# Attention outputs turned, normalised and turned back by VectorE's 32x32 transposes

## Chip, cores and metric

One core of one Trainium2 chip. The metric is the device time of one execution in microseconds (us), a median of several runs. PE is TensorE, ACT is ScalarE, DVE is VectorE, POOL is GpSimd, SP is SyncE, which here only issues DMAs.

## What is computed

One transformer block on 32 batches of 128 tokens with 128 channels: modulated layer norm, self attention with 16 heads of 8 channels, a gated projection added to x, cross attention to 77 context tokens, its projection added to x, and an MLP of 512 hidden channels with its own modulation and gate. Cut to what matters here:

```python
attn_w = softmax(einsum('bhqd,bhkd->bhqk', q, k) * scale)
attn_out = einsum('bhqk,bhkd->bhqd', attn_w, v)            # divided by the sum of the exponentials
x = x + gate_a * (attn_out.transpose(0,2,1,3).reshape(B,N,H) @ W_proj + b_proj)
...                                                        # cross attention the same way, without a gate
x = x + gate_m * (gelu(modulate(ln(x)) @ W_mlp1 + b_mlp1) @ W_mlp2 + b_mlp2)
```

The softmax's division is done after the product with v: the v operand carries a column of ones for each head, so that each head gives 8 unnormalised outputs and the sum of its exponentials.

## The kernel before

**Slots, beats, pairs.** The batches go in 16 pairs. The attention part is a software pipeline of slots -2 to 19. Within a slot `here` is the pair whose self attention begins, `back1` (called `d`) the one before it, whose self attention is finished and projected, `back3` (`e`) the one whose cross attention is finished, `back4` (`z`) the one whose cross output is projected and added. Slots 4 to 13 are a loop of two slots an iteration, the others are written out. Each slot has 8 beats `t`; each engine has its own in-order list of work for each beat, written out by hand in the function `slot` of its block, and engines wait for each other by counting semaphores. After the slots comes the MLP, in 8 groups of 4 batches.

**The scores.** In each beat PE computes one unit of scores (8 heads of one batch) for the row maxima, self attention in beats 0 to 3 and cross attention in beats 4 to 7 (`scores`, L1111), into `ps_max`, which has one buffer. DVE takes the maxima (`maxima`, L736) and PE may write the next unit when DVE is done. In the same way PE computes transposed scores (L1122) into `ps_st`, also a single buffer, and ACT takes their exponentials (L895). PE multiplies the exponentials with v (`values`, L1133) into `ps_o`, one bank for the four units of a pair.

**What is done with `ps_o`.** It holds, for each of 4 groups of 32 partitions, 2 heads times 16 rows (8 outputs, the sum, 7 unused), and 128 queries in the columns of each unit. For self attention of pair `d`:

- beat 1: ACT copies `ps_o` (128x512) to `sum` (`sums`, L916), which frees `ps_o` for the cross units from beat 2 on
- beat 2: PE turns it by four 128x128 transposes into the bank `o_t` (`flip_sums`, L1208)
- beat 3, ahead of that beat's maxima: DVE takes the reciprocal of the sums (L743) and multiplies (L747), from PSUM to `o` with queries in the partitions
- beat 3: PE turns `o` back by two transposes (`flip_out`) into the bank `ob_t`
- beat 4: ACT copies that to `oT` (L923), and PE projects (L1347), DVE adds (L753, `residual`), and after the maxima of beat 5 takes the statistics of the new x (L698), POOL the reciprocal root (L525), and in beat 6 DVE normalises (L714, `normalise`), PE turns it (L1200, `x1_t`), ACT copies it, and in beat 7 PE computes the cross queries (L1221)

Cross attention of pair `e` has the same five steps: sums in beat 5 (after which `ps_o` is free for self units from beat 6 on), `flip_sums` in beat 6, reciprocal and multiply in beat 7 ahead of the maxima, `flip_out` in beat 7, copy to `ocT` in beat 0 of the next slot, then the projection (L1307).

**DMAs.** The q and k operands of the scores are three-way bf16 splits, made by POOL (L530 to L544) and stacked into `qk_st` and `qkc_st` by six DMAs of 128 KB for each pair, issued by SP (L372). Cross queries computed in beat 7 are split, stacked and wanted by PE in beat 4 of the next slot.

**Weights.** The rows of `w_proj` and `w_cproj`, and of two bias columns, are loaded in an order (`o_rows`) that fits the order in which the flips leave the heads; each of these loads is two DMAs.

Of the kernel before, what the change touches and what calls it, by code (L numbers as in the profile page):

```python
# [24 lines left out]
B, T, C = 32, 128, 128  # L25
# [3 lines left out]
G = 2  # L29
# [46 lines left out]
def ring(*streams):  # L76
# [10 lines left out]
        ("max_s0", "here", 2), ("o_t", "back1", 1),  # L87
        ("ob_t", "back1", 2), ("ctx_t", "back1", 0), ("v", "ahead", 1),
        ("max_s1", "here", 0), ("proj", "back1", 2),
        ("kv_c", "back1", 1),  # L90
        ("max_c0", "back2", 0), ("oc_t", "back3", 1), ("x1_t", "back1", 2), ("x_t", "far", 2),
        ("q_c", "back1", 0), ("obc_t", "back3", 1)]
# [91 lines left out]
def block_kernel(nc, x, cond, ctx, w_mod, b_mod, w_qkv, b_qkv, w_proj, b_proj, w_qc, b_qc, w_kvc, b_kvc,  # L184
# [5 lines left out]
    with es:  # L190
# [112 lines left out]
        for name in ("cond_in w_in wm_in wq_in bm_in bd_in b_in bc_in b1_in w12_in wc_in x_in0 x_in1 x_in2 x_in3 x_in4 c_in0 c_in1 c_in2 c_in3 c_in4 z_pool z_dve zq_set zk_set zv_set zvc_set "  # L303
# [4 lines left out]
                     "smax_ps smaxc_ps st_ps stc_ps pv_ps pvc_ps ot_ps obt_ps oct_ps obct_ps "  # L308
# [23 lines left out]
        def hold(eng, name, value):  # L332
# [46 lines left out]
        def _(sp):  # L379
            def o_rows(src):  # L380

                return src.rearrange("(j r m) c -> r j m c", r=2, m=2 * D)

# [20 lines left out]
            for r in range(2):  # L404
                sp.dma_start(wcproj_sb[r * C // 2:(r + 1) * C // 2], o_rows(w_cproj)[r]).then_inc(sems["w_in"], 16)
# [229 lines left out]
        def _(dve):  # L635
# [103 lines left out]
            def attention_out(p, kind, job, ready, rden_name, name, taken):  # L739

                src = ps_misc[BANK[job]][:].rearrange("q (r m x) -> q r m x", r=2 * G, x=2 * D)
                w(dve, ready, p.n + 1)
                nc.vector.reciprocal(att[kind]["rden"][:], src[:, :, :, D]).then_inc(sems[rden_name], 1)  # L743
                if not p.first():
                    w(dve, taken, p.n)
                w(dve, rden_name, p.n + 1)
                nc.vector.tensor_tensor(att[kind]["o"][:], src[:, :, :, 0:D],  # L747
                                        att[kind]["rden"][:].unsqueeze(3).to_broadcast([T, 2 * G, 8, D]),
                                        ALU.mult).then_inc(sems[name], 1)
# [39 lines left out]
            def slot(s):  # L789
                far, a, h, d, f, e, z = (s.pair(n) for n in ("far", "ahead", "here", "back1", "back2", "back3", "back4"))  # L790
                for t in range(BEATS):
# [24 lines left out]

                    if t == 0 and far:
# [45 lines left out]
        def _(act):  # L863
            def o_rows(src):

                return src.rearrange("(j r m) c -> r j m c", r=2, m=2 * D)

# [13 lines left out]
            for r in range(2):  # L881
                act.dma_start(wproj_sb[r * C // 2:(r + 1) * C // 2], o_rows(w_proj)[r]).then_inc(sems["w_in"], 16)
            with nc.allow_non_contiguous_dma(reason="bias columns"):
                for n, (src, at) in enumerate(((b_qkv, 2 * C), (b_kvc, C))):
                    for r in range(2):
                        act.dma_start(bv_sb[r * C // 2:(r + 1) * C // 2, n:n + 1],
                                      o_rows(src[at:at + C].rearrange("(c o) -> c o", o=1))[r]).then_inc(sems["b_in"], 16)
# [15 lines left out]
            def empty_max(p, b, job, ready, dst, name, loaded):  # L903
                w(act, ready, 2 * p.n + b + 1)
                if not p.first():
# [3 lines left out]
                                     ACT.Copy).then_inc(sems[name], 1)  # L909

            def sums(p, kind, src, ready, name, taken):

                w(act, ready, NU * p.n + NU)
                if not p.first():
                    w(act, taken, p.n)
                nc.scalar.activation(att[kind]["sum"][:].rearrange("c b r q -> c (b r q)"), src[:, :],  # L916
                                     ACT.Copy).then_inc(sems[name], 1)
# [38 lines left out]
            def slot(s):  # L956
                a, h, d, f, e, z = (s.pair(n) for n in ("ahead", "here", "back1", "back2", "back3", "back4"))
                for t in range(BEATS):
# [7 lines left out]
                    if t == 0 and z:  # L966
                        copy(ocT[:], ps_misc[BANK["obc_t"]][:, 0:GT], "obct_ps", z, "ocT_set", "projc_ps")
# [27 lines left out]
                    if t == 4 and d:  # L995
                        copy(oT[:], ps_misc[BANK["ob_t"]][:, 0:GT], "obt_ps", d, "oT_set", "proj_ps")
# [29 lines left out]
                    if t == 1 and d:  # L1026
                        sums(d, "s", ps_o, "pv_ps", "sum_set", "ot_ps")
# [15 lines left out]
                    if t == 5 and e:  # L1043
                        sums(e, "c", ps_o, "pvc_ps", "sumc_set", "oct_ps")
# [38 lines left out]
        def _(pe):  # L1083
# [107 lines left out]
            def slot(s):  # L1191
# [10 lines left out]

                def flip(job, p, srcs, ready, counted):

                    dst = bank(s, job)
                    w(pe, ready, p.n + 1)
                    for n, src in enumerate(srcs):
# [232 lines left out]
```

## Time and profile before

| | us |
|---|---|
| median of 3 runs | 406.55 |
| the runs | 403.11, 406.55, 407.51 |
| span of the profiled execution | 401.9 |
| busy in the span: PE, ACT, DVE, POOL | 336.8, 268.8, 257.0, 216.6 |

The span runs from the first instruction to the last of one profiled execution. The time of that execution as the runs count it isn't given; the median of the runs is 4.65 us above its span, the lowest run 1.2 us. Attention fills the span up to about 340 us, the MLP the rest.

### The profile page before, as it was taken

How to read it: one execution, taken by the hardware profiler on the slowest of the kernel's cores; microseconds unless marked ns; L12 is line 12 of the kernel's file. 1: busy time of each engine (PE TensorE's matmuls, PEld its weight loads, DVE VectorE, ACT ScalarE, POOL GpSimd, SP SyncE). 2: the span in 40 equal slices, each digit the busy share in tenths (PEclk: the TensorE clock that was granted, in tenths of full speed). 3: DMA queues.
4: the chain of work that ended last, by engine and by line, in shares of the span. 5: the costliest groups of instructions: out<-in, count | busy, mean ns of one | idle time of the engine just before them, and what ended most of it. 6: DMA issues, size and time to landing. Idle time of an engine off the chain costs nothing.

```text
span 401.9 us, 16368 instructions
## 1 busy us (share of the span) xinstructions
PE 336.8 (84%) x6072; PEld 227.1 (56%) x6072; DVE 257.0 (64%) x650; ACT 268.8 (67%) x523; POOL 216.6 (54%) x494
## 2 busy tenths in 40 slices
PE   3474875989889999999999899988678778999994
PEld 3342553666666767667677677766545434454442
DVE  5754665768779788788887888868625441424401
ACT  1244563868778888887888878877573465677672
POOL 7824475867676686777777777756344210211200
PEclk9997799999999999999999999999997599999998
DMA  5244467253343543435425343353130300001101
GB/s 154 52 105 108 125 151 166 55 136 85 85 97 82 119 106 81 102 85 126 99 68 123 81 116 94 81 123 78 36 82 4 81 2 2 26 26 41 39 26 52
DMA packets 65549, 33.15 MB, mean 82 GB/s; under 512 B 8359, under 2 KB 65255, under 8 KB 65511
## 3 DMA queue, kind: packets, MB, share of 16 engines
q1 hardware_dynamic: 61983, 31.77, 32.7%
q10 hardware_dynamic: 3528, 0.86, 1.1%
q8 instruction: 25, 0.41, 0.4%
q14 instruction: 13, 0.11, 0.1%
HBM read 4.83 MB, written 2.10 MB: 17 GB/s over the span
## 4 chain that ended last, share of the span: by engine, by line
PE 41%; DVE 16%; issue 16%; SPq 9%; DMA 8%; ACT 4%; POOL 2%; ACTq 1%; DVEq 1%; POOLq 0%
PE ps_o L1180 7%; DMA qkc_st<-qkcp 7%; SPq L372 7%; PE ps_o L1133 6%; PE wide L1172 6%; PE wide L1111 5%; DVE x_n L714 3%; PE wide L1122 3%; DVE mxc L736 3%; DVE mx L736 2%; SPq L412 2%; DVE x_stats L698 2%; PE ps_misc L1200 2%; PE ps_misc L1208 2%; PE ps_misc L1221 2%
## 5 line engine op out<-in xcount | busy, mean ns | idle before, releaser
L895 ACT ACTIVATE p_c<-wide 128x1024 f32<-128x1024 f32 x64 | 65.6, 1026 | 36.5 <-PE wide L1122 36.1
L736 DVE TENSOR_REDUCE mx<-wide 128x8 f32<-128x1024 f32 x64 | 78.0, 1218 | 18.4 <-PE wide L1111 18.2
L895 ACT ACTIVATE p_s<-wide 128x1024 f32<-128x1024 f32 x64 | 65.7, 1026 | 11.8 <-PE wide L1122 11.0
L736 DVE TENSOR_REDUCE mxc<-wide 128x8 f32<-128x616 f32 x64 | 51.0, 797 | 27.5 <-PE wide L1111 26.4
L1133 PE MATMUL ps_o<-p_c,vc_m 128*32 128x128 f32 x1024 | 43.0, 287 | 0.8 <-ACT p_c L895 0.6
L1133 PE MATMUL ps_o<-p_s,v_m 128*32 128x128 f32 x1024 | 42.5, 285 | 0.6
L1111 PE MATMUL wide<-qk_st 62*128 62x128 bf16 x512 | 26.5, 225 | 11.6 <-DVE mx L736 9.7
L1111 PE MATMUL wide<-qkc_st 62*128 62x77 bf16 x512 | 20.8, 204 | 14.2 <-DMA qkc_st<-qkcp 13.4
L1111 PEld LDWEIGHTS wide<-qk_st 62*128 62x128 bf16 x512 | 15.1, 97 | 29.3 <-DVE mx L736 23.7
L1133 PEld LDWEIGHTS ps_o<-p_s,v_m 128*32 128x32 f32 x1024 | 25.1, 111 | 8.4 <-issue 3.1
L1172 PE MATMUL wide<-m_nT,w_sb 128*128 128x512 f32 x64 | 29.6, 597 | 0.2 <-DVE mxc L736 0.2
L1133 PEld LDWEIGHTS ps_o<-p_c,vc_m 128*32 128x32 f32 x1024 | 25.0, 112 | 8.0 <-issue 0.9
L1122 PE MATMUL wide<-qkc_st 64*128 64x128 bf16 x512 | 26.0, 221 | 3.6 <-ACT p_c L895 3.3
L1180 PE MATMUL ps_o<-qk_st,w_sb 128*128 128x512 f32 x64 | 28.9, 594 | 0.0
L1122 PE MATMUL wide<-qk_st 64*128 64x128 bf16 x512 | 26.4, 224 | 2.7 <-ACT p_s L895 1.4
L561 POOL CAST nmc<-mxc 128x16 bf16<-128x16 f32 x32 | 6.3, 196 | 40.6 <-issue 26.8
L1111 PEld LDWEIGHTS wide<-qkc_st 62*128 62x128 bf16 x512 | 12.5, 98 | 26.7 <-issue 21.4
L567 POOL TENSOR_TENSOR m_ve<-m_mv,eps_sb 128x4 f32<-128x4 f32 x8 | 1.6, 200 | 47.9 <-DVE m_mv L772 47.9
L753 DVE TENSOR_TENSOR xs<-xs,ps_misc 128x256 f32 (+1 forms) x32 | 13.5, 421 | 17.4 <-PE ps_misc L1347 10.4
L786 DVE TENSOR_TENSOR m_out<-xs,ps_misc 128x512 f32<-128x512 f32 x8 | 5.5, 688 | 29.6 <-PE ps_misc L1188 29.6
L946 ACT ACTIVATE m_y<-ps_o,gb_m,mod 128x128 f32<-128x128 f32 x32 | 12.1, 457 | 18.0 <-PE ps_o L1180 18.0
L525 POOL TENSOR_TENSOR x_rstd<-x_ve,mhalf 128x2 f32<-128x2 f32 x32 | 22.4, 700 | 2.9 <-POOL x_ve L520 0.8
(152 smaller groups left out, 815.5 us busy)
## 6 DMA issues: line engine op xcount, KB each, us to landing
qkc_st<-qkcp SPq DMA_DIRECT2D x96, 128.0 KB, 2.6
qk_st<-qkp SPq DMA_DIRECT2D x94, 128.0 KB, 2.5
out<-m_out SPq DMA_DIRECT2D x8, 256.0 KB, 2.3
xs<-x SPq DMA_DIRECT2D x3, 512.0 KB, 4.9
qk_st<-nmT SPq DMA_DIRECT2D x64, 4.0 KB
qkc_st<-nmcT SPq DMA_DIRECT2D x64, 4.0 KB
ctx_sb<-ctx SPq DMA_DIRECT2D x3, 308.0 KB
w_sb<-L_xcond_W_mlp ACTq DMA_DIRECT2D x2, 256.0 KB, 3.1
```

Of the source, the lines that this page charges most:

```text
L372: queue.dma_start(dst[c:128:ROWSTEP], parts[:].rearrange("c a p t -> c (a p) t")[:, a:b + 4:b + 3 - a]).then_inc(sems[name], 16)
L525: nc.gpsimd.tensor_tensor(L["rstd"][:], L["ve"][:], mhalf[0:L["rows"], 0:G], ALU.pow).then_inc(sems[f"{kind}_rstd_set"], 1)
L714: last = nc.vector.tensor_scalar(L["xn"][:, b], src(b), L["mv"][:, b, 0:1], L["rstd"][:, b:b + 1], ALU.subtract, ALU.mult)
L736: nc.vector.reduce_max(mxt[:, b].rearrange("q (x r) -> q r x", r=2)[:, r], src, AX.X, negate=True).then_inc(sems[done], 1)
L753: nc.vector.tensor_tensor(xs[:, batches(p)], xs[:, batches(p)], ps_misc[BANK[job]][:, 0:GT].rearrange("t (b c) -> t b c", b=G), ALU.add).t ...
L895: nc.scalar.activation(dst[u % 2][:].rearrange("k x q -> k (x q)"), ps_st[:].rearrange("k s x -> k (s x)"), ACT.Exp, scale=SCALE).then_inc ...
L946: last = nc.scalar.activation(m_y[par][:, b * T:(b + 1) * T], ps_y[:, b * T:(b + 1) * T], ACT.Identity, bias=one(gb_m, g, b), scale=one(mo ...
L1111: last = mm(ps_max[:, s_, j * T:j * T + keys], st[p.par][lo:lo + KROWS, m, 0, b * T:(b + 1) * T], st[p.par][lo:lo + KROWS, m, 1, b * T:b * ...
L1122: last = mm(ps_st[:, s_, j * T:(j + 1) * T], st[p.par][lo:lo + HALF, m, 1, b * T:(b + 1) * T], st[p.par][lo:lo + HALF, m, 0, b * T:(b + 1) ...
L1133: last = mm(ps_o[32 * j:32 * j + 32, at:at + T], vt[p.par][:, b, 4 * j + 2 * r + s_], probs[u % 2][:, 4 * s_ + j], start=(s_ == 0), stop=( ...
L1172: mm(ps_h[k], w1_sb[:, k * 128:(k + 1) * 128], m_nT[par][:], start=True, stop=True).then_inc(sems["m_h_ps"], 1)
L1180: last = mm(ps_y[:, :], w2_sb[:, k], hT[par][:, k], start=(k == 0), stop=(k == NF - 1))
```

## The change

DVE takes over the turning. Its transpose instruction turns each 32x32 block by itself and leaves it within its 32 partitions. Since `ps_o` keeps each head's 16 rows within one group of 32 partitions, turning the blocks puts queries in the partitions for four groups of heads at once; after the division the same turn gives channels in the partitions, in the natural order of the heads. Per slot and kind of attention there are now three steps, all on DVE:

- `turn_sums`: one transpose of 128x512 f32 from `ps_o` to `sum` (beat 1 for self, beat 5 for cross, behind that beat's maxima). It frees `ps_o`
- `divide`: reciprocal of 128x32 and multiply of 128x256, both from SBUF (beats 2 and 6, behind the maxima)
- `turn_back`: one transpose of 128x256 f32 from `o` straight to `oT` or `ocT` (beats 3 and 7, ahead of the maxima)

PE loses `flip_sums` and `flip_out`, ACT loses `sums` and the copies to `oT` and `ocT`. Four PSUM jobs (`o_t`, `ob_t`, `oc_t`, `obc_t`) and the waits on their banks are gone. A unit's place in `ps_o` is now (2r+b) instead of (2b+r). `w_proj`, `w_cproj` and the bias columns are loaded in their natural order: 4 DMAs fewer at the start, 3 of them on ACT's queue.

```diff
-            def attention_out(p, kind, job, ready, rden_name, name, taken):
-                src = ps_misc[BANK[job]][:].rearrange("q (r m x) -> q r m x", r=2 * G, x=2 * D)
-                w(dve, ready, p.n + 1)
-                nc.vector.reciprocal(att[kind]["rden"][:], src[:, :, :, D]).then_inc(sems[rden_name], 1)
...
+            def turn_sums(p, kind, ready, name):
+                w(dve, ready, NU * p.n + NU)
+                nc.vector.transpose(att[kind]["sum"][:].rearrange("t (a r s) x -> t a r (s x)", r=2, s=2),
+                                    ps_o[:].rearrange("c (r a q) -> c a r q", r=2, q=32)).then_inc(sems[name], 1)
+            def divide(p, kind, ready, rden_name, name):
+                w(dve, ready, p.n + 1)
+                nc.vector.reciprocal(att[kind]["rden"][:], att[kind]["sum"][:, :, D]).then_inc(sems[rden_name], 1)
+                w(dve, rden_name, p.n + 1)
+                nc.vector.tensor_tensor(att[kind]["o"][:], att[kind]["sum"][:, :, 0:D],
+                                        att[kind]["rden"][:].unsqueeze(2).to_broadcast([128, 2 * G * T // 16, D]),
+                                        ALU.mult).then_inc(sems[name], 1)
+            def turn_back(p, kind, dst, ready, name, taken):
+                w(dve, ready, p.n + 1)
+                if not p.first():
+                    w(dve, taken, p.n)
+                nc.vector.transpose(dst[:], att[kind]["o"][:].rearrange("t m d -> t (m d)")).then_inc(sems[name], 1)
...
                     if t == 3 and d:
-                        attention_out(d, "s", "o_t", "ot_ps", "rden_set", "o_set", "obt_ps")
+                        turn_back(d, "s", oT, "o_set", "oT_set", "proj_ps")
                     if t == 7 and e:
-                        attention_out(e, "c", "oc_t", "oct_ps", "rdenc_set", "oc_set", "obct_ps")
+                        turn_back(e, "c", ocT, "oc_set", "ocT_set", "projc_ps")
...
+                    if t == 1 and d:
+                        turn_sums(d, "s", "pv_ps", "sum_set")
+                    if t == 2 and d:
+                        divide(d, "s", "sum_set", "rden_set", "o_set")
+                    if t == 5 and e:
+                        turn_sums(e, "c", "pvc_ps", "sumc_set")
+                    if t == 6 and e:
+                        divide(e, "c", "sumc_set", "rdenc_set", "oc_set")
...
-                    if t == 0 and z:
-                        copy(ocT[:], ps_misc[BANK["obc_t"]][:, 0:GT], "obct_ps", z, "ocT_set", "projc_ps")
...
-                    if t == 1 and d:
-                        sums(d, "s", ps_o, "pv_ps", "sum_set", "ot_ps")
...
-                at = u * T
+                at = (G * r + b) * T
...
-                    if t == 2 and d:
-                        flip_sums("o_t", "s", d, "sum_set", "ot_ps")
...
-                        flip_out("ob_t", "s", d, "o_set", "obt_ps")
```

## Rows read from the trace of the kernel before

**Rows 1.** The page: busy time (first line), chain that ended last, by engine and line.

```profile
PE 336.8 (84%) x6072; PEld 227.1 (56%) x6072; DVE 257.0 (64%) x650; ACT 268.8 (67%) x523; POOL 216.6 (54%) x494
PE 41%; DVE 16%; issue 16%; SPq 9%; DMA 8%; ACT 4%; POOL 2%; ACTq 1%; DVEq 1%; POOLq 0%
PE ps_o L1180 7%; DMA qkc_st<-qkcp 7%; SPq L372 7%; PE ps_o L1133 6%; PE wide L1172 6%; PE wide L1111 5%; DVE x_n L714 3%; PE wide L1122 3%; DVE mxc L736 3%; DVE mx L736 2%; SPq L412 2%; DVE x_stats L698 2%; PE ps_misc L1200 2%; PE ps_misc L1208 2%; PE ps_misc L1221 2%
```

**Rows 2.** Busy time by stretch: slots 3-5, 6-13, 14-15; stretch, length, engines, clock, DMA.

```profile
78.74:130.59 51.85, 46.19 (x1104) 34.43 (x1092) 40.82 (x97) 40.27 (x80) 36.98 (x85) 1.00 0.41 96
130.59:261.53 130.94, 122.95 (x2916) 91.76 (x2912) 109.39 (x253) 107.63 (x209) 97.14 (x223) 1.00 0.41 98
261.53:295.84 34.31, 28.03 (x683) 20.67 (x672) 22.73 (x47) 24.30 (x47) 19.17 (x49) 1.00 0.32 74
```

**Rows 3.** Timeline, DVE, beat 5 to the next: start, length, line, operation, count, idle before.

```profile
170.19 0.79 DVE L736 TENSOR_REDUCE mxc<-wide 128x8 f32<-128x616 f32 x1
170.90 0.48 DVE L698 BATCH_NORM_STATS2 x_stats<-xs 128x6 f32 x2
172.89 0.60 DVE L714 TENSOR_SCALAR x_n<-xs,x_mv,x_rstd 128x128 f32 x2
173.40 0.36 DVE L743 RECIPROCAL c_rden<-ps_misc 128x32 f32<-128x32 f32 x1
173.87 0.42 DVE L747 TENSOR_TENSOR c_o<-ps_misc,c_rden 128x256 f32<-128x256 f32 x1
174.36 0.80 DVE L736 TENSOR_REDUCE mxc<-wide 128x8 f32<-128x616 f32 x1
175.08 0.75 DVE L714 TENSOR_SCALAR ctx_n<-ctx_sb,ctx_mv,ctx_rstd 77x128 f32 x2
...
180.66 1.23 DVE L736 TENSOR_REDUCE mx<-wide 128x8 f32<-128x1024 f32 x1 [0.52 <-PE wide L1111]
182.05 0.36 DVE L743 RECIPROCAL s_rden<-ps_misc 128x32 f32<-128x32 f32 x1 [0.17 <-PE ps_misc L1208]
182.85 1.22 DVE L736 TENSOR_REDUCE mx<-wide 128x8 f32<-128x1024 f32 x1
184.79 0.80 DVE L736 TENSOR_REDUCE mxc<-wide 128x8 f32<-128x616 f32 x1 [0.72 <-PE wide L1111]
186.21 0.42 DVE L753 TENSOR_TENSOR xs<-xs,ps_misc 128x256 f32 x1 [0.62 <-PE ps_misc L1347]
```

**Rows 4.** Timeline, PE, the same slot: where PE waited for the maxima and for DMA.

```profile
177.91 0.40 PE L1111 MATMUL wide<-qk_st 62*128 62x128 bf16 x8 [0.26 <-DVE mx L736]
180.19 0.40 PE L1111 MATMUL wide<-qk_st 62*128 62x128 bf16 x8 [0.22 <-DVE mx L736]
...
184.34 0.32 PE L1111 MATMUL wide<-qkc_st 62*128 62x77 bf16 x8 [0.20 <-DMA qkc_st<-qkcp]
```

**Rows 5.** Groups by line: name, shapes, count, busy us, mean ns, idle us before.

```profile
L736 DVE TENSOR_REDUCE mx<-wide 128x8 f32<-128x1024 f32 x64 | 78.0, 1218 | 18.4 <-PE wide L1111 18.2
L786 DVE TENSOR_TENSOR m_out<-xs,ps_misc 128x512 f32<-128x512 f32 x8 | 5.5, 688 | 29.6 <-PE ps_misc L1188 29.6
L638 DVE MEMSET qk_st<- 128x1024 uint32 x2 | 1.8, 912 | 1.2 <-PEq L1430 1.0 <-issue 0.2
```

**Rows 6.** Busy time by stretch, early slots, for the granted clock; columns as in rows 2.

```profile
45.30:66.00 20.70, 14.42 (x253) 9.19 (x245) 13.64 (x30) 11.77 (x25) 15.94 (x35) 1.00 0.61 138
66.00:68.00 2.00, 0.39 (x17) 0.36 (x21) 0.02 (x1) 0.00 (x0) 1.05 (x1) 1.00 0.49 114
68.00:70.00 2.00, 1.80 (x49) 1.27 (x46) 1.80 (x3) 0.49 (x2) 0.00 (x0) 0.62 0.52 122
```

**Rows 7.** Timeline, all engines, slots 18 and 19, the last pair's cross attention output.

```profile
333.16 0.64 PE L1133 MATMUL ps_o<-p_c,vc_m 128*32 128x128 f32 x16 [0.57 <-ACT p_c L895]
...
335.58 0.60 ACT L916 ACTIVATE c_sum<-ps_o 128x512 f32<-128x512 f32 x1
...
336.32 0.63 PE L1208 MATMUL ps_misc<-ident,c_sum 128*128 128x128 f32 x4 [0.60 <-ACT c_sum L916]
```

More of the change, by code:

```diff
@@ L86 @@
         ("qk", "ahead", 0),
-        ("max_s0", "here", 2), ("o_t", "back1", 1),
-        ("ob_t", "back1", 2), ("ctx_t", "back1", 0), ("v", "ahead", 1),
+        ("max_s0", "here", 2),
+        ("ctx_t", "back1", 0), ("v", "ahead", 1),
         ("max_s1", "here", 0), ("proj", "back1", 2),
         ("kv_c", "back1", 1),
-        ("max_c0", "back2", 0), ("oc_t", "back3", 1), ("x1_t", "back1", 2), ("x_t", "far", 2),
-        ("q_c", "back1", 0), ("obc_t", "back3", 1)]
+        ("max_c0", "back2", 0), ("x1_t", "back1", 2), ("x_t", "far", 2),
+        ("q_c", "back1", 0)]
 BANK = {name: bank for name, _, bank in MISC}
@@ L403, in _ @@
             load_x(1)
-            for r in range(2):
-                sp.dma_start(wcproj_sb[r * C // 2:(r + 1) * C // 2], o_rows(w_cproj)[r]).then_inc(sems["w_in"], 16)
+            sp.dma_start(wcproj_sb[:], w_cproj).then_inc(sems["w_in"], 16)
             for dst, src in ((wqc_sb, w_qc), (wkvc_sb, w_kvc)):
@@ L908, in empty_max @@
                 nc.scalar.activation(dst[:, b], ps_misc[BANK[job]][:].bitcast(bf16)[0:2 * H, 0:T],
[L909 to L916, printed above, removed]
                                      ACT.Copy).then_inc(sems[name], 1)
@@ L1201, in transposed @@
                     last.then_inc(sems[counted], 1)
[L1203 to L1207, printed above, removed]
-                        last = tr(dst[:, n * 128:(n + 1) * 128], src, ident[:])
-                    last.then_inc(sems[counted], 1)
-                def flip_sums(job, kind, p, ready, counted):
-                    flip(job, p, [att[kind]["sum"][:, b, r] for b in range(G) for r in range(2)], ready, counted)
-                def flip_out(job, kind, p, ready, counted):
-                    flip(job, p, [att[kind]["o"][:, 2 * b:2 * b + 2].rearrange("q r m d -> q (r m d)") for b in range(G)],
-                         ready, counted)
                 def project(job, p, weights, src, ready, counted, cols=GT):
@@ L1364, in slot @@
                         max_t("max_c0", f, 0, nmc, "nmc_set", "mtc_ps")
-                    if t == 6 and e:
-                        flip_sums("oc_t", "c", e, "sumc_set", "oct_ps")
                     if t == 6 and far:
@@ L1373, in slot @@
                         project("q_c", d, wdh[:, 2], x1T[:], "x1T_set", "qc_ps")
-                    if t == 7 and e:
-                        flip_out("obc_t", "c", e, "oc_set", "obct_ps")
                     if h and h.first() and t < 2:
```

40 lines of the change are left out of this document (13 added, 27 removed).

## The prediction

> **What bounds the kernel now.** I read the page first. PE is busiest by far [rows 1], so a change that takes work off PE looks welcome. But the chain that ended last has only 41% on PE, and three things around it that aren't PE's arithmetic: DVE's maxima and statistics, SP's issue of the `qkc_st` stack, and that stack's flight. So I cut the span into slots by the starts of `sums` and asked for the busy time of each stretch. Slots 6 to 13 take 130.94 us, 16.37 us each; in such a slot PE is busy 15.37 us, DVE 13.67, ACT 13.45, POOL 12.1 [rows 2]. PE idles 1.0 us a slot and DVE 2.7.
>
> Whether PE's busy time sets that 16.37 I read from the timelines of DVE and of PE over one slot. DVE runs from the residual of beat 4 (the last row is the next slot's; this slot's lies 16.36 us earlier, at 169.85) to the maxima of beat 1, which end 0.52 ahead of the 180.66 row, at 180.14, with nothing between its operations but short waits on itself; neighbours overlap by 0.07 to 0.09 us, as 170.19 + 0.79 against 170.90 shows. After it come 0.52, 0.17, 0.72 and 0.62 us of waiting for PE [rows 3]. PE in turn waits for DVE's maxima at 177.91 and 180.19, and barely for the DMA at 184.34 [rows 4]. The reader is to see a chain that passes from DVE to PE and back: scores can't be written before the maxima of the unit ahead are taken, since `ps_max` has one buffer, and for 10.3 of 16.4 us DVE has no gap in which more work would be free. PE is nearly full, but over that stretch it is full because it has the time. A second loop is as long: cross queries in beat 7, split, six DMAs, scores in beat 4 of the next slot; the 0.20 us wait on DMA [rows 4] says that it closes at nearly the same moment.
>
> **What the change takes away.** On PE twelve transposes a slot: four take 0.63 us [rows 7], so 1.9 us of busy time. On ACT two copies of 0.60 us [rows 7] and two of half that size, 0.3 to 0.6 us each: about 2 us. On DVE the wait of 0.17 us for the flip [rows 3]. On POOL nothing. Neither PE's nor ACT's work lies on the path of the 10.3 us; what it would be worth there I count as nothing, because what bounds there is DVE. The cover for that is DVE's own queue; if it weren't full, the two `flip_sums` on PE would be worth 0.6 us each.
>
> **What it adds on DVE.** No row shows a DVE transpose. Nearest is a DVE operation from PSUM with the same 512 elements a partition, 688 ns (L786); the maxima with 1024 take 1218 ns [rows 5], so an element costs (1218-688)/512 = 1.04 ns and an operation 157 ns. By that `turn_sums` is 0.69 us and `turn_back` with 256 elements 0.42, the time of the multiply and residual of that size [rows 3]. Less the overlap of 0.08 they cost the queue 0.61 and 0.34 us. Ends of the range: a memset does 1024 words in 912 ns [rows 5], 0.89 ns each with nothing for the start, so 0.46 and 0.23 us, which I take as the low end; if a 4-byte element needs two passes, the 1024-element reduction gives 1.22 us, and the same 1.04 ns gives 0.69 us for 256 elements. I take the middle, since element counts and source are the same. `divide` keeps two operations; their source moves from PSUM to SBUF. They take 0.36 and 0.42 now; I leave them so. `turn_back` waits on the multiply directly in front of it in beat 6 to 7 and beat 2 to 3 (only `residual`-like work could stand between, and there is none), 0.1 us as between reciprocal and multiply (173.40 + 0.36 against 173.87).
>
> The Trainium skill (Vector Engine (DVE) Microarchitecture Reference, section 3.8) says that the transposing front end sustains one element per cycle and lane, and its page VectorE: DVE Perf Modes (section on the TRN2 errata) gives 120 cycles and one per element from PSUM, 58 from SBUF, at 0.96 GHz. By these figures, an estimate, the two would be 0.66 and 0.33 us in place of 0.69 and 0.42, and the forecast about 2 us lower. No run here shows it yet; the nearest row, 688 ns, is 30 ns above the page's figure for its size.
>
> **One slot walked through.** Cross half, beats 5 to 7 [rows 3]: `turn_sums` comes between the maxima at 170.19 and the statistics at 170.90. Its input, PE's last cross product, is queued on PE right behind the scores whose maxima DVE spends 0.79 us on, so I take it as ready when they end, and everything behind moves by 0.61: statistics, POOL's root, `x1_n` at 172.89, the cross queries. Reciprocal and multiply then fill 173.40 to 174.29 as before, and where the next maxima stood at 174.36 `turn_back` stands until 174.73: 0.37 more. From 175.08 to 180.14 DVE is full, so the 0.98 us arrive whole at beat 1. Self half: `turn_sums` follows the maxima of beat 1 and takes 0.61 us, and there the queue had a gap of 0.52 while PE makes the next scores: 0.01 to 0.1 more, counted as 0. PE's first cross product of beat 2 waits for it (`sum_set`), queued in front of the rest of that beat, but it is ready within 0.05 us of when ACT's copy would let it go. The reciprocal no longer waits 0.17, and `turn_back` comes before the maxima of 182.85: 182.05-0.24+0.36+0.10+0.42+0.10+0.34 = 183.13, so 0.28 more. The gaps of 0.72 and 0.62 are PE's own scores and projection, unchanged. Sum: 0.98 + 0 + 0.28 = 1.26 us, a slot of 17.6 us with DVE busy about 15.6.
>
> **The sum.** Slots 6 to 13: 8 x 1.26 = 10.1 us. Slots 3 to 5 and 14 to 15 take 17.2 us on average [rows 2]; in them I take the DMA loop as the longer one (SP's issue and the flight of `qkc_st` have 7% of the chain each, [rows 1]), which hides the self half, but `turn_sums` of cross attention stands in front of the cross queries and so inside that loop: 5 x 0.61 = 3.0. Slots 16 and 17, the same: 1.2. Slots 1 and 2 have only the self half, ahead of a DMA wait: 0. Slot 18 gives back: the last product ends at 333.80, but the last `c_sum` comes on ACT only at 335.58, behind work of the MLP, and PE waits 0.60 us for it and turns for 0.63 [rows 7]. DVE, idle there, needs 0.69 + 0.36 + 0.42 + 0.42 and three waits of 0.1, 2.2 us from 333.80, and has `ocT` at 336.0. PE's wait of 0.60, its flips of 0.63 and 0.3 and, in front of the projection, about another 0.5 of waiting for the copy go: 2.0 us less. At the start four DMA issues go; ACT's queue has 1% of the chain, 4 us at the most [rows 1], and the loads on it that the first steps need stand ahead of those: 0. Total 10.1 + 3.0 + 1.2 - 2.0 = +12.3: a span of 401.9 + 12.3 = 414.2 us. The median of the runs lies 4.65 above the span of the profiled one, so 406.55 + 12.3, about 419 us. POOL and SP get no work; with 1.26 us more in each slot their queues only wait longer.
>
> **Rivals.**
> (a) The transposes need two passes. `turn_sums` and `turn_back` cost 0.53 and 0.27 us more, 1.6 a slot for both halves: over the 14 slots 3 to 16 +22, so 441 us. For it: reciprocals of 32 elements in 0.36 us show that a DVE operation can cost far more than 1 ns an element. Against: nothing in the rows.
> (b) DVE and POOL get in each other's way. Two `ctx_n` of 128 elements take 0.75 us at 175.08, while POOL works, against 0.60 for two `x_n` [rows 3]. The multiply now reads two SBUF operands; 0.15 us on each of six operations a slot is up to 0.9, x 14 = +13: 432. The Trainium skill (GPSIMD Engine Reference, its specifications) has such contention for DVE operations with two SBUF inputs; by its rule the multiply, but not the transposes, is slowed. The 0.75 us is consistent with that, no more.
> (c) The clock. PE goes from 15.4 busy of 16.4 us to 13.5 of 17.6, 77%. The clock fell to 1.2 GHz after a stretch in which PE did 0.39 us in 2.0, and held at 2.4 with 14.42 busy in 20.70 us, 70% [rows 6]. No gap over 1.5 us is to come in a slot, so it should hold. If not, PE's operations take up to twice as long, some +1.5 us a slot: 14 x 1.5 = +21: 440.
> (d) The transposes are cheap (0.46 and 0.23 us). Then a slot grows by 1.26 - 0.23 - 2 x 0.19 = 0.65 us, and the cross half's share in the DMA loop is 0.38: 5.2 + 5 x 0.38 + 2 x 0.38 - 2.0 = +5.9: 412. If PE's relief hides some of that, as much as 0.3 us a slot, it is 409.
> (e) It gets faster: DVE's work fits in its gaps, and PE is what bounds. Place: the gaps of 0.52, 0.17, 0.72 and 0.62 us, 2.0 us a slot, against 1.9 added. Price: the four-transpose flip of each half leaves the chain; `ps_misc L1208` has 2% of it, 8 us [rows 1], and with the tail's 2 that is 396. It decides if the new work can start in the gaps; for three of the four it can't, since in the hand-written order the operation behind the gap is the one that waits.
>
> **Chances.** Forecast with its own range 414 to 425: 0.60. (a) 0.07, (b) 0.08, (c) 0.05, (d) 0.12, (e) 0.08. The measurement tells about 1% from no change, so faster is below 402.5 and slower above 410.6 us. Faster: (e), 0.08. Same: half of (d), and what of the forecast and of (b) PE's relief might bring there, 0.11 in all. Slower: 0.81. Range for 8 in 10: from 408, the low side of (d), to 432, the end of (b), leaving out (a), (c) and (e).
>
> **What would show it.** In the profile after: slots of 17.6 us in the loop; DVE transposes of 0.69 and 0.42 us; DVE busy 15.6 us a slot, PE about 13.5; PE's waits for `mx` and `mxc` grown by over 1 us a slot; the 0.52 us gap gone, those of 0.6 to 0.7 kept; clock 1.00 there. Wrong if transposes are far from 0.69, if the slot stays at 16.4 with full DVE (then DVE wasn't on the path), or if the DMA wait in beat 4 grows instead.

## The result and the profile after

The median of 4 runs is 438.88 us (436.53 to 439.64), against 404.83 for 4 runs of the kernel before: a ratio of 1.083 (1.076 to 1.089). The change costs 34 us where 12.3 were forecast, and the time lies outside the range. The profiled execution has a span of 437.3 us, 35.4 more than the 401.9 before. A few runs of each kernel fall into a slower state: the ratios leave them out, the medians don't, and the profiled execution of `self_only` is one of them.

The page of the kernel after: busy time, the granted clock in 40 slices, the chain by engine, and four of the costliest groups (line, engine, operation, count | busy us, mean ns | idle before).

```profile
PE 340.3 (78%) x5880; PEld 221.8 (51%) x5880; DVE 288.1 (66%) x714; ACT 247.2 (57%) x459; POOL 220.8 (50%) x494
PEclk9999796989896988989889898989996567899999
PE 44%; DVE 20%; issue 11%; SPq 10%; DMA 8%; ACT 3%; ACTq 1%; POOL 1%; DVEq 1%; POOLq 0%
L731 DVE TENSOR_REDUCE mxc<-wide 128x8 f32<-128x616 f32 x64 | 50.9, 795 | 32.6 <-PE wide L1102 32.4
L1191 PE MATMUL ps_misc<-ident,x_n 128*128 128x128 f32 x64 | 15.0, 328 | 32.0 <-DVE x_n L709 32.0
L1102 PE MATMUL wide<-qk_st 62*128 62x128 bf16 x512 | 28.4, 237 | 13.9 <-DVE mx L731 12.2
L1010 ACT ACTIVATE x1T<-ps_misc 128x256 f32<-128x256 f32 x16 | 6.2, 384 | 37.8 <-PE ps_misc L1191 37.8
```

Set against [rows 1], two lines don't fit a plain loss on VectorE. PE has 192 instructions fewer and is busy 3.5 us longer, so what is left of its work runs slower: the clock row dips to 8 in about half of the slices of the loop, where the page of before has a 9 in each slice there. And PE idles 32.0 us for `x_n`, the normalised input that it turns; before it was 6.5 us on the same line (L1200 there). So I looked at beat 6, where DVE normalises x1. The lines of the new and the kept operations, DVE:

```profile
L737 DVE STREAM_TRANSPOSE c_sum<-ps_o 128x512 f32<-128x512 f32 x16 | 11.3, 708 | 7.8 <-PE ps_o L1124 7.8
L737 DVE STREAM_TRANSPOSE s_sum<-ps_o 128x512 f32<-128x512 f32 x16 | 11.3, 706 | 0.5 <-PE ps_o L1124 0.5
L745 DVE TENSOR_TENSOR s_o<-s_sum,s_rden 128x256 f32<-128x256 f32 x16 | 8.0, 502 | 0.5
L745 DVE TENSOR_TENSOR c_o<-c_sum,c_rden 128x256 f32<-128x256 f32 x16 | 7.3, 457 | 0.5
L754 DVE STREAM_TRANSPOSE oT<-s_o 128x256 f32<-128x256 f32 x16 | 7.1, 445 | 0.5
```

The prices are those of the forecast: 0.71 and 0.44 us for 0.69 and 0.42, so the sum must have failed elsewhere. The timeline of DVE over beats 5 to 7 of one slot of the loop, which answers to [rows 3] (start, length, line, operation, idle before):

```profile
222.25 0.79 DVE L731 TENSOR_REDUCE mxc<-wide 128x8 f32<-128x616 f32 x1
222.96 0.70 DVE L737 STREAM_TRANSPOSE c_sum<-ps_o 128x512 f32<-128x512 f32 x1
223.59 0.44 DVE L693 BATCH_NORM_STATS2 x_stats<-xs 128x6 f32 x2
...
224.84 0.79 DVE L731 TENSOR_REDUCE mxc<-wide 128x8 f32<-128x616 f32 x1
225.54 0.34 DVE L743 RECIPROCAL c_rden<-c_sum 128x32 f32<-128x32 f32 x1
225.92 0.42 DVE L745 TENSOR_TENSOR c_o<-c_sum,c_rden 128x256 f32<-128x256 f32 x1
226.26 0.60 DVE L709 TENSOR_SCALAR x_n<-xs,x_mv,x_rstd 128x128 f32 x2
226.78 0.44 DVE L754 STREAM_TRANSPOSE ocT<-c_o 128x256 f32<-128x256 f32 x1
227.96 0.80 DVE L731 TENSOR_REDUCE mxc<-wide 128x8 f32<-128x616 f32 x1 [0.75 <-PE wide L1102]
...
231.04 1.22 DVE L731 TENSOR_REDUCE mx<-wide 128x8 f32<-128x1024 f32 x1 [0.99 <-PE wide L1102]
```

The cross reciprocal and multiply stand ahead of x1's normalisation at 226.26. Before, that normalisation came first (172.89) and they followed (173.40, [rows 3]). What this does to PE, in its timeline over the same beats:

```profile
224.97 0.44 PE L1191 MATMUL ps_misc<-ident,x_n 128*128 128x128 f32 x2 [0.46 <-DVE x_n L709]
227.00 0.51 PE L1191 MATMUL ps_misc<-ident,x_n 128*128 128x128 f32 x2 [1.60 <-DVE x_n L709]
227.45 0.44 PE L1102 MATMUL wide<-qkc_st 62*128 62x77 bf16 x8
...
228.25 1.08 PE L1124 MATMUL ps_o<-p_s,v_m 128*32 128x128 f32 x16
229.26 1.22 PE L1197 MATMUL ps_misc<-x1T,wdh 128*128 128x256 f32 x2
```

And the windows over them (stretch, length, then busy time of PE, weight loads, DVE, ACT, POOL, granted clock, DMA share, GB/s):

```profile
224.00:226.00 2.00, 0.95 (x19) 0.48 (x11) 1.82 (x8) 1.06 (x2) 1.34 (x4) 1.00 0.36 78
226.00:228.00 2.00, 0.99 (x16) 0.76 (x18) 1.25 (x5) 0.45 (x2) 1.67 (x5) 0.80 0.38 103
228.00:230.00 2.00, 2.00 (x24) 1.15 (x20) 1.86 (x7) 1.11 (x2) 0.79 (x3) 0.50 0.02 4
```

PE waits 0.46 and 1.60 us (in every second slot of the loop 0.43 and 2.06 or 2.07), works half of 4 us, and the granted clock is 0.50, the 1.2 GHz level, in the next stretch. The product of beat 6 then takes 1.08 us and the cross queries 1.22; at full clock the same operations take 0.65 and 0.70. These two alone lose 0.95 us in a slot; their neighbours are slowed too. DVE waits in turn: 0.75 us for the scores at 227.45, which stand on PE behind the flip of x1, and at 231.04 another 0.99 for scores that stand behind the queries.

By slots, from the starts of POOL's gate product (`wg`, one for each of 16 slots), the 35.4 us lie: 0.8 in slots 1 and 2, 8.5 in 3 to 5, 20.3 in 6 to 13, -0.1 in 14 and 15, 6.0 behind. A slot of the loop takes about 18.85 us.

### The profile page after: what moved, and what is told of

Its sections match the earlier page's. It is cut to its first block, busy times and chain, and to the rows that moved or that the text cites. A ratio compares the mean times of both kernels' runs of the same rounds, so it can differ in the third digit from the quotient of the medians.

```text
span 437.3 us, 15855 instructions
## 1 busy us (share of the span) xinstructions
PE 340.3 (78%) x5880; PEld 221.8 (51%) x5880; DVE 288.1 (66%) x714; ACT 247.2 (57%) x459; POOL 220.8 (50%) x494
## 4 chain that ended last, share of the span: by engine, by line
PE 44%; DVE 20%; issue 11%; SPq 10%; DMA 8%; ACT 3%; ACTq 1%; POOL 1%; DVEq 1%; POOLq 0%
PE ps_o L1124 8%; DMA qkc_st<-qkcp 7%; SPq L372 7%; PE wide L1163 7%; PE ps_o L1171 6%; DVE mxc L731 4%; PE wide L1102 4%; DVE mx L731 4%; PE wide L1113 4%; PE ps_misc L1197 3%; DVE x_n L709 3%; SPq L407 2%; PE ps_misc L1191 2%; PE ps_misc L1320 2%; DVE x_stats L693 2%
## 5 line engine op out<-in xcount | busy, mean ns | idle before, releaser
L1124 PE MATMUL ps_o<-p_s,v_m 128*32 128x128 f32 x1024 | 48.4, 315 | 0.0
L1124 PE MATMUL ps_o<-p_c,vc_m 128*32 128x128 f32 x1024 | 44.3, 294 | 1.0 <-ACT p_c L902 0.6
L1191 PE MATMUL ps_misc<-ident,x_n 128*128 128x128 f32 x64 | 15.0, 328 | 32.0 <-DVE x_n L709 32.0
L1102 PE MATMUL wide<-qk_st 62*128 62x128 bf16 x512 | 28.4, 237 | 13.9 <-DVE mx L731 12.2
L1102 PEld LDWEIGHTS wide<-qk_st 62*128 62x128 bf16 x512 | 16.2, 101 | 36.7 <-DVE mx L731 24.7
L1163 PE MATMUL wide<-m_nT,w_sb 128*128 128x512 f32 x64 | 33.0, 657 | 1.6 <-DVE mxc L731 1.6
L1124 PEld LDWEIGHTS ps_o<-p_s,v_m 128*32 128x32 f32 x1024 | 27.6, 121 | 8.7 <-issue 3.1
L1113 PE MATMUL wide<-qk_st 64*128 64x128 bf16 x512 | 29.7, 244 | 2.2 <-DMA qk_st<-nmT 1.1
L1102 PEld LDWEIGHTS wide<-qkc_st 62*128 62x128 bf16 x512 | 13.1, 102 | 32.6 <-issue 20.2
L1010 ACT ACTIVATE x1T<-ps_misc 128x256 f32<-128x256 f32 x16 | 6.2, 384 | 37.8 <-PE ps_misc L1191 37.8
L1191 PEld LDWEIGHTS ps_misc<-ident,x_n 128*128 128x128 f32 x64 | 7.2, 156 | 38.5 <-issue 31.8
```

Of the source, the lines that this page charges most:

```text
L1102: last = mm(ps_max[:, s_, j * T:j * T + keys], st[p.par][lo:lo + KROWS, m, 0, b * T:(b + 1) * T], st[p.par][lo:lo + KROWS, m, 1, b * T:b * ...
L1113: last = mm(ps_st[:, s_, j * T:(j + 1) * T], st[p.par][lo:lo + HALF, m, 1, b * T:(b + 1) * T], st[p.par][lo:lo + HALF, m, 0, b * T:(b + 1) ...
L1124: last = mm(ps_o[32 * j:32 * j + 32, at:at + T], vt[p.par][:, b, 4 * j + 2 * r + s_], probs[u % 2][:, 4 * s_ + j], start=(s_ == 0), stop=( ...
L1163: mm(ps_h[k], w1_sb[:, k * 128:(k + 1) * 128], m_nT[par][:], start=True, stop=True).then_inc(sems["m_h_ps"], 1)
L1191: last = tr(dst[:, at + b * rows:at + (b + 1) * rows], ln[kind]["xn"][:, b], ident[0:rows, 0:rows])
```

## The experiments

A slot is the mean distance of `wg` starts over slots 6 to 12 (before: 16.37), in `late_divide` without two slots that are named there; the clock is the granted clock over 130 to 270 us (before: 1.00). Ratios are against the kernel before on the same chip, with their 95% interval.

**Which half.** `self_only` keeps the cross half as before and turns only self attention on DVE; `cross_only` is the reverse. Cut to its core, the edit of the first against the kernel after is:

```diff
                     if t == 7 and e:
-                        turn_back(e, "c", ocT, "oc_set", "ocT_set", "projc_ps")
+                        attention_out(e, "c", "oc_t", "oct_ps", "rdenc_set", "oc_set", "obct_ps")
...
-                    if t == 5 and e:
-                        turn_sums(e, "c", "pvc_ps", "sumc_set")
-                    if t == 6 and e:
-                        divide(e, "c", "sumc_set", "rdenc_set", "oc_set")
```

> Only the self half goes by VectorE's transposes; the cross half as in the kernel before. Theory A: the self half's turn of the sums fills a gap of 0.52 us and its other two steps cost 0.3 us, no clock drop: slot 16.4 to 16.7 us, 403 to 410 us. Theory B: half of the whole loss, about 421 us.

> Only the cross half goes by VectorE's transposes; the self half as in the kernel before. Theory A: nearly all of the loss is here, with the clock falling once a slot: slot 18.3 to 18.9 us, 428 to 437 us. Theory B: half of the loss, about 421 us.

`self_only`: 408.16 us, 1.005 (1.001 to 1.009), slot 16.5, clock 1.00. `cross_only`: 441.53 us, 1.087 (1.081 to 1.093), above the 428 to 437 expected; slot 19.1, clock 0.89, and PE's second wait for x1 is 1.59 or 2.06 us. All that can be measured of the loss but a half per cent is in the cross half. Of the self half the walk expected 0.28 us a slot; it is about 0.1.

**The place of the division.** `late_divide` only moves the cross reciprocal and multiply behind x1's normalisation, where they stood before:

```diff
                     if t == 5 and e:
                         turn_sums(e, "c", "pvc_ps", "sumc_set")
-                    if t == 6 and e:
-                        divide(e, "c", "sumc_set", "rdenc_set", "oc_set")
...
                         normalise("x1", d, x_of(d), "x1t_ps")
+                    if t == 6 and e:
+                        divide(e, "c", "sumc_set", "rdenc_set", "oc_set")
```

> The changed kernel with one edit: in beat 6 the cross half's reciprocal and multiply come behind the normalisation of x1, not ahead of it. Theory A (the place): the divide holds x1's normalisation back by 0.8 us, PE stands idle over 2 us in beat 6, its granted clock falls to 1.2 GHz once a slot, and the cross queries are late twice over; then the idle falls to about 1.2 us, the clock stays at 1.00 and a slot takes about 17.6 us instead of 18.85: 415 to 421 us. Theory B (the load): the 2.1 us a slot more on VectorE cost what they are wherever they stand: the slot stays at 18.8 and the time at 434 to 439 us.

417.01 us (415.87 to 418.66), 1.027 (1.022 to 1.031), slot 17.17, clock 0.99. Two operations moved by one place give back 22 of the 34 us. Its DVE timeline in beats 6 and 7:

```profile
194.46 0.80 DVE L731 TENSOR_REDUCE mxc<-wide 128x8 f32<-128x616 f32 x1
195.17 0.70 DVE L709 TENSOR_SCALAR x_n<-xs,x_mv,x_rstd 128x128 f32 x2
195.79 0.34 DVE L743 RECIPROCAL c_rden<-c_sum 128x32 f32<-128x32 f32 x1
196.16 0.44 DVE L745 TENSOR_TENSOR c_o<-c_sum,c_rden 128x256 f32<-128x256 f32 x1
196.64 0.45 DVE L754 STREAM_TRANSPOSE ocT<-c_o 128x256 f32<-128x256 f32 x1
197.01 0.76 DVE L731 TENSOR_REDUCE mxc<-wide 128x8 f32<-128x616 f32 x1
```

The normalisation starts 0.71 us behind the maxima's start, in the kernel after 1.42. PE's timeline shows the same at the flip of x1, in two slots:

```profile
213.19 0.41 PE L1191 MATMUL ps_misc<-ident,x_n 128*128 128x128 f32 x2 [0.87 <-DVE x_n L709]
214.58 1.12 PE L1197 MATMUL ps_misc<-x1T,wdh 128*128 128x256 f32 x2
...
231.90 0.41 PE L1191 MATMUL ps_misc<-ident,x_n 128*128 128x128 f32 x2 [0.98 <-DVE x_n L709]
233.28 0.70 PE L1197 MATMUL ps_misc<-x1T,wdh 128*128 128x256 f32 x2
```

Waits of 0.87 to 0.98 us instead of 1.60 to 2.07. The first of the two rows of queries shows that this kernel is still near the edge: there they take 1.12 us, at a clock of 0.68 and then 0.50 until 218 us. It is the only slot of the loop in which that happens, and it and the next one are 17.6 and 18.3 us long; the others are 17.17. With the same wait of 0.87 us the clock stayed up in the other slots.

**The clock by itself.** `warm` is the kernel after with 12 transposes of the identity into the x1 bank, written over by the real ones, ahead of the flip of x1. They keep PE at work and change no order on DVE.

```diff
+                        for _ in range(12):
+                            tr(ps_misc[BANK["x1_t"]][:, 0:128], ident[:], ident[:])
```

> The changed kernel with twelve 128x128 transposes of the identity more on TensorE in beat 6, in front of x1's transposes, into columns that those overwrite; some 1.5 us of the time in which TensorE waits for x1. Nothing else is changed. Theory A: the granted clock stays at 1.00 in the loop, the matmuls behind keep their fast times (products 0.64 us, cross queries 0.70 instead of 1.08 and 1.22) and a slot is shorter by 0.9 to 1.2 us: 422 to 427 us. Theory B, in which the clock is only a symptom off the path: 434 to 439 us.

427.38 us (424.4 to 429.39), 1.054 (1.046 to 1.061), slot 17.9, clock 1.00. The time is at the upper end of what theory A gave. PE's timeline:

```profile
216.91 0.44 PE L1191 MATMUL ps_misc<-ident,x_n 128*128 128x128 f32 x2 [0.46 <-DVE x_n L709]
217.18 1.47 PE L1343 MATMUL ps_misc<-ident 128*128 128x128 f32 x12
219.32 0.44 PE L1191 MATMUL ps_misc<-ident,x_n 128*128 128x128 f32 x2 [0.66 <-DVE x_n L709]
...
220.16 0.65 PE L1124 MATMUL ps_o<-p_s,v_m 128*32 128x128 f32 x16
```

x1 comes no sooner, but the product behind it takes 0.65 us again. Useless work on PE makes the kernel 11.5 us faster: 18.85 - 17.9 = 0.95 us a slot is the clock's share. I read such differences to 0.05 us at best, and that the two slow operations above add up to the same is partly chance, since their neighbours are slowed as well.

`late_warm` is `late_divide` with the same 12 transposes.

> The kernel of the run late_divide with the twelve transposes of the run warm. In late_divide the loop already runs at clock 1.00; only slots 1 to 5 and the last ones show a lower one. If the clock is no longer part of the loss in the loop: 412 to 418 us, within 1% of late_divide. If what stays of the loss (0.8 us a slot) were a matter of TensorE's activity: 405 to 409 us.

419.53 us, 1.035 (1.030 to 1.040), 1.5 us above the range expected; slot 17.17, clock 1.00. With the division in its late place the clock has no share left to give in the loop (17.17 in both), and the 12 transposes themselves cost nothing there; what they cost, 2.5 us, lies in the slots ahead of it. So `warm` against `late_divide` is a fair reading of the order: 17.9 - 17.17 = 0.73 us a slot, close to the 0.71 by which the normalisation comes later.

**Do the missing flips let the clock fall?** `warm_few` puts only four transposes, as many as `flip_sums` had, into beat 6 ahead of the flip of x, with the rest as after:

```diff
+                    if t == 6 and d:
+                        w(pe, "x1_set", d.n + 1)
+                        for _ in range(4):
+                            tr(ps_misc[BANK["x1_t"]][:, 0:128], ident[:], ident[:])
```

> The changed kernel with four 128x128 transposes of the identity more on TensorE in beat 6, 0.6 us of work at the place where the cross half's flips of the sums stood before, in columns that x1's transposes overwrite. TensorE still waits 1.6 to 2 us for x1 behind them. Theory C (the clock falls because the flips no longer stand in beat 6; before_delay kept them, waited 1.5 us and kept the clock): the clock stays at 1.00 in most slots of the loop, slot 17.9 us, 423 to 428 us as in the run warm. Theory A alone (the wait for x1 is what lets it fall, whatever stands around it): 433 to 438 us.

437.07 us (432.28 to 438.37), 1.079 (1.074 to 1.085), slot 18.4, clock 0.95; the profiled execution is the lowest of the four. The 0.46 us wait is gone and the one of 1.59 to 2.06 us for x1 stays. What follows it is mixed. In slots 3 to 13 the queries take 0.70 us five times and 0.96 to 1.22 us six times. Two slots of the loop, PE:

```profile
188.87 0.41 PE L1191 MATMUL ps_misc<-ident,x_n 128*128 128x128 f32 x2 [1.59 <-DVE x_n L709]
190.25 0.70 PE L1197 MATMUL ps_misc<-x1T,wdh 128*128 128x256 f32 x2
...
225.17 0.54 PE L1191 MATMUL ps_misc<-ident,x_n 128*128 128x128 f32 x2 [1.59 <-DVE x_n L709]
227.44 1.22 PE L1197 MATMUL ps_misc<-x1T,wdh 128*128 128x256 f32 x2
```

The wait is the same and the outcome isn't. Putting back work of that size holds the clock in some slots only, and the medians are 1.8 us apart with overlapping runs. `before_delay` tries it from the other side: all of PE's work as before, and two scratch transposes of 128x512 on DVE, one in beat 5 and one in beat 6, ahead of x1's statistics and normalisation.

```diff
+                    if t == 5 and e:
+                        nc.vector.transpose(idle[1][:], idle[0][:])
+                    if t == 6 and e:
+                        nc.vector.transpose(idle[2][:], idle[0][:])
```

> The kernel before, with all of TensorE's and ScalarE's turning, and two VectorE transposes of 128x512 from one scratch tile to others added: one in beat 5 ahead of x1's statistics, one in beat 6 ahead of x1's normalisation, 0.6 us of queue each. Nothing reads them. Theory A (late x1 is enough): TensorE waits over 1.5 us for x1 in beat 6, and with the slot 1.2 to 1.4 us longer the clock falls in many slots: 17.6 to 18.8 us a slot, 424 to 438 us. Theory C (the clock falls because TensorE has lost its transposes): here it keeps them, the clock stays at 1.00 and only the 1.24 us a slot are lost: 17.6 us a slot, 419 to 424 us.

421.33 us (419.88 to 421.9), 1.041 (1.033 to 1.048), slot 17.4, clock 1.00.

```profile
216.30 0.41 PE L1206 MATMUL ps_misc<-ident,x_n 128*128 128x128 f32 x2 [1.47 <-DVE x_n L716]
217.68 0.70 PE L1227 MATMUL ps_misc<-x1T,wdh 128*128 128x256 f32 x2
```

PE waits 1.47 us for x1 and the queries still take 0.70; so it is, with waits of 1.43 to 1.50 us, in ten of slots 3 to 13, and in slot 4 they take 1.05. The delay alone, with no change in what PE and ACT do, costs 16 us: DVE's work ahead of x1 is on the path. That it kept the clock fits the theory that the missing flips let it fall; `warm_few`, with four transposes back, holds it only in part. The length of the wait alone doesn't decide it either. The kernel after itself shows a longer one that was borne, in slot 14 (and the same in slot 15):

```profile
302.74 0.41 PE L1191 MATMUL ps_misc<-ident,x_n 128*128 128x128 f32 x2 [1.85 <-DVE x_n L709]
...
304.12 0.70 PE L1197 MATMUL ps_misc<-x1T,wdh 128*128 128x256 f32 x2
```

The shorter wait ahead of it is missing there, and over the two stretches of 2 us from 300 us PE is busy 0.89 and 1.26, at a clock of 1.00.

**What PE's and ACT's relief is worth.** `late_tiny` is `late_divide` with both transposes cut to 32 columns, so that most of the attention outputs stay unturned. The edit of one of them:

```diff
-                nc.vector.transpose(att[kind]["sum"][:].rearrange("t (a r s) x -> t a r (s x)", r=2, s=2),
-                                    ps_o[:].rearrange("c (r a q) -> c a r q", r=2, q=32)).then_inc(sems[name], 1)
+                nc.vector.transpose(att[kind]["sum"][:, 0:2].rearrange("t m x -> t (m x)"),
+                                    ps_o[:, 0:32]).then_inc(sems[name], 1)
```

> The kernel of the run late_divide with both VectorE transposes cut to one 32-column block, so most of the attention outputs are not turned and the output is not the reference's (the tiles they leave unwritten are set to 1 at the start). All waits and all else stay. It shows what the work taken off TensorE and ScalarE is worth when the new work is nearly free. Theory A (VectorE is the bound in the slot, with the DMA loop close behind): slot 15.8 to 16.3 us, 396 to 404 us. Theory D (the relief is worth nothing even then, the DMA loop holds the slot): 16.3 to 16.6 us, 404 to 408 us.

407.28 us (405.69 to 410.49), 1.007 (1.003 to 1.011), slot 16.46. The four short transposes still take 0.21 us each on DVE. By that an estimate is 4 x (0.21 - 0.08) = 0.5 us more in DVE's queue, less the 0.17 us wait that is gone, where the slot grew by 0.1. So by this estimate a relief worth some 0.2 us a slot may be hidden here. Beyond that, 1.9 us of PE and 2 us of ACT a slot less bring no gain that the transposes' price ate up.

**How far it can be mended.** `late_both` moves the cross `turn_sums` too, behind x1's statistics:

```diff
-                    if t == 5 and e:
-                        turn_sums(e, "c", "pvc_ps", "sumc_set")
...
                         aggregate("x1", d)
+                    if t == 5 and e:
+                        turn_sums(e, "c", "pvc_ps", "sumc_set")
```

> The kernel of the run late_divide with the cross half's turn of the sums put behind x1's statistics in beat 5 as well. x1 is ready 0.6 us earlier, but TensorE's first self product of beat 6 waits for ps_o to be free. Theory A (VectorE is full over the stretch, so only its total counts): slot 17.1 to 17.3 us as in late_divide, 415 to 419 us. Rival (the path through x1 still sets the slot): 16.6 to 16.9 us, 408 to 413 us.

413.87 us, 1.024 (1.017 to 1.032), between the two ranges expected; slot 17.06: 0.1 a slot less than `late_divide`, the rest of the 3 us in the written-out slots, of which the last `wg` interval is 14.5 us instead of 15.8.

`self_gap` is `self_only` with `turn_back` moved from beat 3 to beat 4, where DVE waited for PE:

```diff
-                    if t == 3 and d:
+                    if t == 4 and d:
                         turn_back(d, "s", oT, "o_set", "oT_set", "proj_ps")
```

> The kernel of the run self_only (self half by VectorE's transposes, cross half as before), with the self half's turn back moved from ahead of beat 3's maxima to ahead of beat 4's, where VectorE has a gap of 0.6 us waiting for scores. Theory A (VectorE's place in the chain is what costs): 0.3 us a slot less than self_only, 16.1 us, 402 to 405 us. Rival (the DMA loop is now the longer one): 16.35 us and 406 to 409 us as in self_only.

405.98 us (403.56 to 408.33), 1.003 (0.999 to 1.007), slot 16.0 and 16.4 in turn: no different from before. `self_pool` has in addition the self multiply on POOL, `all_moved` is `late_both` with both of these edits.

```diff
+                    w(pool, "rden_set", d.n + 1)
+                    nc.gpsimd.tensor_tensor(att["s"]["o"][:], att["s"]["sum"][:, :, 0:D],
+                                            att["s"]["rden"][:].unsqueeze(2).to_broadcast([128, 2 * G * T // 16, D]),
+                                            ALU.mult).then_inc(sems["o_set"], 1)
```

> The kernel of the run self_gap with the self half's multiply on GpSimd behind the gated projection weights. Theory A: VectorE has 0.4 us less in beat 2, but the DMA loop was already the longer one in every other slot of self_gap: slot 15.9 to 16.1 us, 400 to 405 us. Rival (the split of q and k, 0.7 us later on GpSimd, now makes the scores wait): 406 to 412 us.

> The kernel of the run late_both, with the self half's turn back ahead of beat 4's maxima (as in self_gap) and the self half's multiply on GpSimd behind the gated projection weights, 0.7 us there. Theory A (VectorE's load in the stretches where it is full is the bound): 0.4 us less from the multiply and 0.3 from the gap, slot 16.3 to 16.5 us, 400 to 405 us with the shorter tail. Rival (the DMA loop holds 16.4 us, and GpSimd's split of q and k comes later): 404 to 410 us.

407.7 us, 1.007 (1.003 to 1.011), slot 16.4 and 16.6; and 413.54 us, 1.020 (1.017 to 1.024), slot about 17.0. The multiply off DVE gains nothing; both missed the 400 to 405 us hoped for, and `all_moved` lies above its rival's 404 to 410 as well. No version beat the kernel before, and the closest are those that leave the cross half alone.

## Why the prediction was wrong in size

**The direction and its reason held.** DVE is on the path, PE's busy time isn't: `before_delay` shows the first, `late_tiny`, but for some 0.2 us a slot, the second. The transposes cost 0.706 and 0.445 us. The Trainium skill (VectorE: DVE Perf Modes, section on the TRN2 errata) would give 0.66 and 0.33, an estimate; for the 256-element transpose the measurement decides against it, and the rate read from the maxima's rows was nearer. The gap of 0.52 us of beat 2 is gone: `s_sum` starts at 215.64 and the maxima behind it at 216.33.

**The step that failed is in the slot walk**: "Reciprocal and multiply then fill 173.40 to 174.29 as before". Their place isn't as before. The diff puts `divide` in beat 6 directly behind the maxima and ahead of `normalise("x1")`; I had written its beat down right and then left it, in the walk, at the time where the old rows show it. So x1's normalisation was moved by 0.61 in the sum and by 0.61 + 0.71 on the chip. The sign that I gave for it, PE's waits for the row maxima grown by over 1 us a slot, fails with it. They grow from 10.1 us in all to 15.8, while those for x1 grow by 25.5. In `late_divide`, which has the order that I walked, they grow to 26.1, the 1.0 us a slot that was forecast.

`late_divide` also measures the walk by itself: 17.17 us a slot where 17.6 was forecast, so 0.8 more for 1.26, and 417.01 us beside the 419. That the two times are so near is partly luck: slots 1 to 15 cost 10.4 us, where the walk has 13.1, and what lies behind the last `wg` costs 4.6 more where -0.8 was forecast.

**From the same step the clock was dismissed.** Rival (c) named this mechanism and had a chance of 0.05, because "No gap over 1.5 us is to come in a slot". With the true order there are gaps of 0.46 and then 1.6 to 2.07 us. Its 440 us is near the measured 438.88 by luck: it put up to 1.5 us a slot on the clock and left the order as it was. Per slot of the loop the runs show:

| | us a slot | shown by |
|---|---|---|
| turning on DVE, division in its late place | 0.8 | `late_divide` 17.17 against 16.37 |
| division ahead of x1's normalisation | 0.73 | `warm` 17.9 against 17.17 |
| clock at 1.2 GHz once a slot | 0.95 | kernel after 18.85 against `warm` 17.9 |
| sum | 2.5 | forecast 1.26 |

The first line answers to the forecast's 1.26 and is smaller; the other two come from the one place in DVE's queue. The self half's 0.28 is about 0.1: in a slot of `self_only` the maxima of beat 3 start 6.37 us behind those of beat 0 (179.34 to 185.71), before 6.22 (176.63 to 182.85), so 0.15 later, and the wait for PE behind them, which I had left unchanged, is 0.55 us where 0.72 stood. The cross half has 17.17 - 16.5 = 0.7 for 0.98.

**Slots 3 to 5 and the tail.** The DMA loop was to hide the rest in slots 3 to 5, at 0.61 a slot; they lost 8.5 us in the kernel after and 2.6 in `late_divide`, where 1.8 was forecast. In slot 18 the saving of 2.0 us is real where the clock there is full. From the end of the last cross product to the projection it was 5.76 us before (333.80 to 339.56, [rows 7] and L1307). `late_divide`, PE:

```profile
350.20 0.64 PE L1124 MATMUL ps_o<-p_c,vc_m 128*32 128x128 f32 x16 [0.57 <-ACT p_c L902]
350.78 3.70 PE L1163 MATMUL wide<-m_nT,w_sb 128*128 128x512 f32 x8
...
354.53 0.61 PE L1283 MATMUL ps_misc<-wcproj_sb,ocT 128*32 128x128 f32 x16
```

350.84 to 354.53 is 3.69 us, 2.07 less. The kernel after:

```profile
367.63 1.08 PE L1124 MATMUL ps_o<-p_c,vc_m 128*32 128x128 f32 x16 [0.57 <-ACT p_c L902]
368.64 6.33 PE L1163 MATMUL wide<-m_nT,w_sb 128*128 128x512 f32 x8
374.89 0.29 PE L1279 MATMUL ps_misc<-g_rows,ones 128*32 128x256 bf16 x4
375.01 0.61 PE L1283 MATMUL ps_misc<-wcproj_sb,ocT 128*32 128x128 f32 x16
```

Here `ocT` is there at 370.82, and PE comes to it only at 375.01, behind an MLP layer that takes 6.33 us for 3.70, at a granted clock of 0.58 for 1.00. Ahead of that, in the stretch from the last `wg` to the last maxima, the loss is 3.6 us in the kernel after and 4.3 in `late_divide`, at a granted clock of 0.67 and 0.61 against 0.76 before; from there to the end of the last cross product it is another 1.9 and 2.4 us, at 0.80 and 0.77 against 1.00. The forecast had no term for the clock there, though the kernel before was already below full in those slots. That this clock is the cause of those losses wasn't tried by itself.

**The other rivals.** (a) is false by the prices. (b) is there but small: 0.077 and 0.032 us on the two multiplies, 0.1 a slot (0.2 in `late_divide`). (d) and (e) are false by the prices and by `late_tiny`.

**Open**: what exactly separates the waits that the clock bore from those after which it fell. Waits of 0.42 to 0.47 and then 1.59 to 2.07 us were followed by slow queries in all of slots 3 to 13 of the kernel after, but only in nine of those eleven in `cross_only`; a single one of 1.85 us was borne. The runs give these cases, and no rule. Open, too, is why slots 3 to 5 lose 2.6 us even in `late_divide`.

## What to carry to other kernels

When work is moved between engines, write down the new queue of the receiving engine line by line from the diff before reading any time from the old trace; an operation that keeps its name need not keep its neighbour, and here one place was worth 22 of 34 us. Put what the next engine waits for ahead of what has slack (x1's normalisation before the cross division). And when PE is relieved while its inputs come later, check its clock: here it was busy 3.5 us longer with 192 instructions fewer.

## What the runs showed of the hardware

- The granted clock of PE can fall in every slot after two short waits (0.46 and 1.6 to 2.1 us, PE busy 0.95 and 0.99 of two stretches of 2 us), and rises again within the slot. The low that I had read before came after a much emptier stretch [rows 6]. A single wait of 1.85 us, in slots 14 and 15 of the same kernel, was followed by a clock of 1.00.
- Work whose result is thrown away pays: 12 transposes, 1.47 us of PE a slot, bought 0.95 us a slot in `warm`.
- DVE's transpose of 4-byte elements takes 706 to 708 ns for 512 elements a partition from PSUM (700 to 702 from SBUF in `before_delay`), 434 to 445 ns for 256 from SBUF and 207 to 212 ns for 32 in `late_tiny`, over all 32x32 blocks in one instruction. From 256 to 512 elements that is nearly the rate of its reductions.
- POOL's subtraction `qkr` takes 1323 ns on average, 1159 before, and DVE's self multiply 502 ns for 425, now that it reads two SBUF operands. The Trainium skill (GPSIMD Engine Reference, section 1) names contention of POOL with DVE instructions with two SBUF inputs; the rows agree, and put it at 0.1 to 0.2 us for one operation.
